# Shifting the projection weight groups, the second input tile and the buffers behind them by multiples of 64 bytes in on-chip memory

## What is computed

```
q = (draft_hidden @ Wq.T).reshape(bsz, draft_len, H, HD)          # H 16, HD 128
kv_in = jnp.concatenate([context_hidden, draft_hidden], axis=1)
k = (kv_in @ Wk.T).reshape(bsz, total_len, KVH, HD)               # KVH 4
v = (kv_in @ Wv.T).reshape(bsz, total_len, KVH, HD).transpose(0, 2, 1, 3)
... rms norm, rotary turn, softmax(q k / sqrt(HD)) v ...
return attn @ Wo.T
...
g = jax.nn.silu(jnp.einsum('td,edf->etf', x, w_gate))
y = jnp.einsum('etf,efd->etd', g * u, w_down)
...
x = x + jnp.tanh(g_xattn[0]) * _L0_xattn_ref(_layernorm(x), ctx_2048, ...)
x = x + jnp.tanh(g_ffn[0]) * _L0_ffn_ref(_layernorm(x), ...)
```

## Time and profile before

| what | value |
|---|---|
| median of 3 runs | 1233.72 us (1233.03 to 1234.22) |
| the profiled execution | 1232.97 us |
| its span, first to last instruction | 1231.2 us, so 1.8 us lie around it |
| granted TensorE clock, mean | 0.998 |
| PE busy | 1206.6 us, 98% of the span |
| PEld / DVE / ACT / POOL busy | 92% / 82% / 72% / 75% |

### The profile page before, as it was taken

How to read it: one execution, slowest core, us unless ns; L and a number is a source line. 1 busy time by engine, 2 the same in 40 slices (tenths; PEclk the granted TensorE clock), 3 DMA queues, 4 the chain that set the end, 5 groups by cost and what they waited for, 6 DMA issues and landing times.

```text
span 1231.2 us, 31490 instructions
## 1 busy us (share of the span) xinstructions
PE 1206.6 (98%) x8781; PEld 1137.8 (92%) x8782; DVE 1009.8 (82%) x2992; ACT 884.6 (72%) x3754; POOL 922.4 (75%) x1124
## 2 busy tenths in 40 slices
PE   6899999999999999999999999999999999999998
PEld 3788999999999999999999999999999899999997
DVE  8788888888888888888888888888888677777443
ACT  7978777777777777777777777777777546666322
POOL 2778888888888888888888888888887425555654
PEclk9999999999999999999999999999999999999999
DMA  6634233322222222223333333222236536554574
GB/s 179 198 116 130 73 109 104 100 90 90 90 90 90 94 90 94 90 90 96 115 107 98 103 108 118 90 75 75 75 110 214 191 108 185 168 156 148 187 232 155
DMA packets 128792, 148.57 MB, mean 121 GB/s; under 512 B 13824, under 2 KB 108288, under 8 KB 127968
## 3 DMA queue, kind: packets, MB, share of 16 engines
q1 hardware_dynamic: 122256, 130.16, 34.9%
q0 software_dynamic: 6480, 17.77, 3.9%
HBM read 66.93 MB, written 80.76 MB: 120 GB/s over the span
## 4 chain that ended last, share of the span: by engine, by line
PE 92%; DVE 3%; ACT 2%; DMA 1%; issue 1%; SPq 0%; another core or an unknown queue 0%; POOL 0%; DVEq 0%; POOLq 0%; ACTq 0%
PE b_kv L1711 14%; PE b_q L1697 14%; PE b_o L1795 13%; PE b_sc L1769 9%; PE b_aT L1784 9%; PE b_pT L1777 5%; PE b_qT L1758 4%; PE b_q L2031 3%; PE b_kv L2031 3%; PE b_kT L1754 2%; PE b_q L1828 2%; PE b_kT L1828 2%; PE b_aT L1946 1%; PE b_pT L2048 1%; PE b_aT L2048 1%; PE b_o L1747 1%
## 5 line engine op out<-in xcount | busy, mean ns | idle before, releaser
L1711 PE MATMUL b_kv<-w_group,kv_in_hi 128*128 128x256 f32 x992 | 205.6, 305 | 0.0
L957 ACT ACTIVATE probs<-b_sc,neg_max 128x128 f32<-128x128 f32 x512 | 180.0, 371 | 0.1
L747 POOL TENSOR_TENSOR qk_r<-qk_me,minus_half 128x6 f32<-128x6 f32 x128 | 172.2, 1345 | 10.1
L751 POOL TENSOR_TENSOR q_rot<-q_rot,q_sin 128x512 f32<-128x512 f32 x128 | 164.4, 1284 | 6.9 <-DVE q_sin L1273 1.9
L1711 PEld LDWEIGHTS b_kv<-w_group,kv_in_hi 128*128 128x128 f32 x992 | 161.8, 190 | 6.7 <-issue 0.4
L1697 PE MATMUL b_q<-w_group,kv_in_hi 128*128 128x512 f32 x496 | 164.8, 413 | 0.0
L951 ACT ACTIVATE pT<-b_pT 128x512 f32<-128x512 f32 x128 | 76.6, 599 | 99.6 <-PE b_pT L1777 97.5
L1795 PE MATMUL b_o<-wo_hi,aT_hi 128*128 128x256 f32 x480 | 143.5, 299 | 0.1
L1769 PE MATMUL b_sc<-kT,qT 128*128 128x128 f32 x1024 | 135.9, 275 | 6.2 <-ACT qT L946 4.2
L754 POOL TENSOR_TENSOR q_rot<-q_rot,qk_r 128x512 f32<-128x512 f32 x128 | 133.4, 1043 | 10.0
L1711 PE MATMUL b_kv<-w_group,kv_in_lo 128*128 128x256 f32 x496 | 139.6, 282 | 0.0
(11 more groups left out here) (309 smaller groups left out, 3942.2 us busy)
## 6 DMA issues: line engine op xcount, KB each, us to landing
xs_scratch<-zeros SPq DMA_DIRECT2D x34, 1032.0 KB, 6.3
s_in<-xs_scratch SPq DMA_DIRECT2D x71, 129.0 KB
yT_scratch<-yT SPq DMA_DIRECT2D x32, 256.0 KB
yS<-yT_scratch SPq DMA_DIRECT2D x32, 256.0 KB
routed<-ys_scratch SPq DMA_DIRECT2D x32, 256.0 KB, 3.4
w_hi_all<-w_scratch SPq DMA_DIRECT2D x3, 1536.0 KB, 13.2
x_in<-in_x SPq DMA_DIRECT2D x32, 128.0 KB, 2.3
ctx_raw<-in_ctxT SPq DMA_DIRECT2D x32, 128.0 KB, 2.6
```

What stands on the lines that cost most here:

```text
L747: nc.gpsimd.tensor_tensor(qk_r[g % 2][:], qk_me[:], minus_half[:, 0:REP + NB], ALU.pow).then_inc(r_ready, 1)
L751: nc.gpsimd.tensor_tensor(q_rot[g % 2][:], q_rot[g % 2][:], q_sin[g % 2][:], ALU.add) \
L957: last = nc.scalar.activation(probs[:, j, :], b_sc[:, j * P:(j + 1) * P], ACT.Exp, bias=neg_max[g % 2][:, j:j + 1], accum_out=row_sum[g % ...
L1711: last = nc.tensor.matmul(b_kv[:, s * 2 * HD:(s + 1) * 2 * HD], kv_in[p][a][:, c, 2 * s:2 * s + 2, :], wkv_of(b, c)[:, g % KVH, :], start= ...
```

## The change

It inserts unused bytes at three places, and thereby moves every buffer behind them. `GROUP_W` adds 16 elements (64 bytes) to each of the four groups of `w_group`, `kv_gap` puts 64 bytes between the two buffers of `kv_in`, and `kv_end` 64 bytes behind the second.

```diff
+GROUP_W = 2 * DC * (REP * HD + 2 * HD) + 16
...
-        w_group = sb("w_group", [P, KVH, 2 * DC * (REP * HD + 2 * HD)], F32R)
-        back_at = [phase_at[0] + 4 * (KVH - 1) * 2 * DC * (REP * HD + 2 * HD)]
+        w_group = sb("w_group", [P, KVH, GROUP_W], F32R)
+        back_at = [phase_at[0] + 4 * (KVH - 1) * GROUP_W]
...
-        kv_in = [parts(f"kv_in{p}", [P, DC, 4, S]) for p in range(2)]
+        kv_in = [parts("kv_in0", [P, DC, 4, S])]
+        kv_gap = sb("kv_gap", [P, 16], F32)
+        kv_in.append(parts("kv_in1", [P, DC, 4, S]))
         ring_end = cursor[0]
+        kv_end = sb("kv_end", [P, 16], F32)
         free_at = list(cursor)
...
-            phase_size = 2 * DC * KVH * (REP * HD + 2 * HD)
+            phase_size = KVH * GROUP_W
```

## The result

The changed kernel is slower: 1235.87 us (median of 20 runs, 1234.05 to 1238.53) against 1233.51 for the kernel before (20 runs, 1232.28 to 1236.66). The ratio is 1.0018, with a 95% interval of 1.0012 to 1.0025, so the loss is about 2.2 us, or 0.18%. The forecast was a gain of 3.4 us, and rival A, with a loss, is on the right side.

A forecast was written before the change was run, and what follows sets the result against it. TensorE was taken to bound the kernel. The key/value projection's -3.4 us was the only nonzero term, so the median would go from 1233.72 to 1230.3 us, with a range of 1226.0 to 1239.5.

The forecast's parts named there:

- rival A: Output projection loses its good place, +6.6 us, key/value projection gains 1.7; together +4.9, or 1238.6 us; chance 0.25.
- What bounds the kernel: Attention phase: TensorE busy for 847.27 of 850 us, so time per matmul is time of the kernel.
- L1711, -3.4 us: Key/value projection: 62 of 124 groups leave a distance that is a multiple of 128, gaining 0.055 us each.
- distance: Stationary operand's place minus the moving one's, modulo 512; claimed to set a loop's pitch, 0.119 to 0.120 against 0.114 us.
- The forecast is wrong at its root if two groups with the same distance differ: Sign to look for in the key/value projection's timeline: then the distance isn't the variable.
- L1795, nothing: Output projection: distance goes from 320 to 448 and the pitch stays 0.114 us; other end 6.6 us lost.
- L1697, zero within 1.6 us: Query projection, 512 moving columns: new distances cost nothing, with ends of 1.6 us either way.
- The 352-column rows: Feed-forward loops used as evidence for the query projection: all distances cost the same within 1%.
- Turns, scores, feed-forward part: Zero each: turns keep 0.22 and 0.44 us, scores' operands move together, feed-forward at most 0.7 us gained.
- rival B: Whole kernel: places don't matter and the 0.005 us pitch difference has another cause; 1233.7 us; chance 0.22.
- the rule of the Trainium skill: TensorE: loading the next weights takes no bandwidth from the running matmul, so no distance matters; sum zero, 1233.7 us.

The follow-up runs named there:

- e2: Kernel before, padded so that projection weights and input tiles keep their places, while output weights and all behind move (output projection at distance 448); ratio 0.9984.
- e8: Kernel before with the moves of e2 and, as in e5, both input tiles 192 bytes further on; ratio 1.0018.
- e1: Kernel before with only the 64 bytes per projection weight group, padding returning every other buffer to its old place modulo 512; ratio 1.0004.
- e7: Kernel before with 64 bytes ahead of the projection weights, moving all places but no distance of the projections; attention stage 947.2 us against 947.5.
- e5: Kernel before with both input tiles 192 bytes further on, all behind at its old place modulo 512; ratio 0.9994.
- e6: Kernel before with both input tiles 448 bytes further on, all behind at its old place modulo 512; ratio 0.9994.
- x1: Kernel before with the last head's turn done twice ahead of each output projection, no address changed; attention stage 962.1 us against 947.5.

## Why the prediction was wrong

- **What bounds the kernel**: right. TensorE is busy for 847.30 of 850 us in the attention stage against 847.27 before, so the loss there is pitch and not waiting.
- **L1711, -3.4 us**: right in sign; -2.5 measured, so the forecast was 0.9 us too large. The pattern was right in three of four kinds that were to become fast: parity 1 with g 0 and 2, and parity 0 with g 3, end at 113.3 to 113.9 ns. Parity 0 with g 1, at the same distance 192 as parity 1 with g 2, ends at 118.0. "The forecast is wrong at its root if two groups with the same distance differ" is what happened.
- **L1795, nothing**: the step that failed. "I take nothing, since 448 differs from 320 by exactly 128" cost +3.3 us (+3.4 in the second trace). Both ends were stated, 0 and 6.6, and the truth lies in the middle, at a pitch of about 117.7 ns that no loop showed as its settled one before.
- **Rival A** had the right loop and sign, for a wrong reason. It put the loss on the distance 448. e2 has this distance and no loss. What cost the time is that the loops ahead changed: with its own operands in place, the output projection turns slow when only the input tiles move (e2 against e8) or only the weight groups (e1).
- **L1697, zero within 1.6 us**: +1.0, inside the ends. The 352-column rows didn't show it.
- **Turns, scores, feed-forward part**: zero was right within the 0.5 us that the traces differ by anyway in the first two. L1832 and L1950 moved by less than 0.6 us. The slots vary by 2.8 us between executions, more than any effect of their places that I could have seen.
- **No effect of places at all** (rival B, and the rule of the Trainium skill, "TensorE: Matmul & The Clock Gate", Step-by-step, that a weight load takes nothing from the running matmul): that no place matters is refuted. e7 moves both operands of the key/value loop by 64 bytes and e5 only one of them by 192, and the loop's sums are 3.2 us apart. So what the prediction drew from the rule, a sum of zero, fails. That it is the weight load which holds up the matmul isn't shown, since no run has these matmuls without loads beside them.
- Sum by measured terms: -2.5 + 1.0 + 3.3 = +1.8 us, and the attention stage is 1.4 to 2.0 us longer, against 2.2 us by the ratio.

The deeper fault is that I took the settled pitch of three loops for a function of one number. The trace of before would have warned me: the same L1711 goes through pitches of 117 and 118 before it settles at 120, and of L1697 the pitches vary within one group.

**Open.** What one loop hands to the next. That it is a state within TensorE is an inference; a fixed meeting with other engines' traffic is the rival that is left. The traces show most weight loads starting 2 to 5 ns behind a matmul in either pace. The first pitch of a group doesn't tell the pace either: in the changed kernel 15 groups that begin with 201 ns end fast and 45 slow. "Behind a fast key/value group the output projection is slow" holds in 25 of 28 groups in e1, in all 44 in the changed kernel and in all 20 in e8, but in none of 36 in e5. So it isn't the pace alone that is handed on, and I can't say from a layout which pace a loop will take.

## What to carry to other kernels

Where TensorE is busy without a gap and weight loads run beside float32 matmuls, compare the pitch of loops of equal shape in the timeline. Here a difference of 5% came with where the two operands lie relative to each other, modulo 256 bytes, and a distance of a multiple of 256 was the worst. But don't price a shift from one loop's pitch. At odd multiples of 64 the 256-column loops here had two settled paces, and which one a group took changed with what ran ahead, so move one buffer at a time, look at the same loop in every kind of unit, and expect single gains not to add. The best layout of this study (e2, 0.9984) kept the projection weights and the input tiles in place and moved the output weights and what lies behind, and it leaves the worst loop as it was.

## What the runs showed of the hardware

- At full granted clock a 256-column matmul of the split loops, with its weight load beside it, settled at one of three pitches: about 113.4, about 117.7, or 120.0 ns. At distances 0 and 256 it went towards 120.0, at odd multiples of 64 it was one of the first two and nothing between. At 128 and 384 it didn't settle and swung between 112 and 124 ns around 118.5.
- Equal distances modulo 256 gave equal loops within 0.1 us in 124 groups (e5 and e6), and moving both operands by 64 bytes gave the same loop within 0.1 us (e7).
- One extra matmul of 0.109 us ahead took 33 of 120 groups of a loop that doesn't use its result from the fast pace to the slow one, 1.38 to 1.42 us each, at unchanged addresses (x1).
- Turns of 128 columns kept 0.11 us each at the three distances that occurred: 0 before, 384 after, 64 in e7.
